# An audio tower on one core: the expert gate's product with its operands exchanged

## The reference

```python
x = hidden_states.reshape(n, d)                  # n = 8000 frames, d = 192, layer-normed
scores = jax.nn.sigmoid(x @ gate_weight.T)       # 8000 x 16
capacity = math.ceil(n / E * TOP_K)              # 1000 frames for each of 16 experts
topk_score, topk_ids = jax.lax.top_k(scores.T, capacity)
xg = x[topk_ids]
gate = jax.nn.silu(jnp.einsum('ecd,efd->ecf', xg, Wg))
up = jnp.einsum('ecd,efd->ecf', xg, Wu)
out = jnp.einsum('ecf,edf->ecd', gate * up, Wd)
out = out * topk_score[..., None]
y = jnp.zeros((n, d), x.dtype).at[topk_ids.reshape(-1)].add(out.reshape(-1, d))
```

## Time and profile before

| | |
|---|---|
| median of 3 runs | 2032.82 us (2029.86 to 2035.56) |
| profiled execution | 2029.4 us, of which 2027.7 us span from the first to the last instruction |
| mean granted TensorE clock | 0.987 |
| the tower in it | to about 1096.5 us |
| a round with all five stages | 31.33 us |

### The profile page before, as it was taken

The page is one execution under the profiler, slowest core; times in us unless marked ns, Lnnn a source line. Parts: engine busy times, 40 slices in busy tenths (PEclk is TensorE's granted clock), DMA queues, the critical chain, the costliest instruction groups (busy, mean ns, idle before and its releaser), DMA issues. The chain is left out here.

```text
span 2027.7 us, 47599 instructions
## 1 busy us (share of the span) xinstructions
PE 1883.7 (93%) x13428; PEld 1605.2 (79%) x13428; DVE 1496.1 (74%) x3956; ACT 1243.6 (61%) x2924; POOL 745.1 (37%) x587
## 2 busy tenths in 40 slices
PE   3899999999999999999985889899999999999997
PEld 2688888888888878888874777688888888888886
DVE  1578788788787887877874777678877778877753
ACT  2687878878878788787862222255555555555553
POOL 0022222122222222222220000357767777776763
PEclk9899999999999999999997999899999999999999
DMA  5556667666666666666664333425544555544452
GB/s 158 151 160 182 179 171 192 167 179 180 171 182 175 173 189 168 178 179 170 188 169 114 108 100 102 115 47 112 97 83 82 96 87 94 109 91 82 84 99 21
DMA packets 318050, 272.97 MB, mean 135 GB/s; under 512 B 80732, under 2 KB 305326, under 8 KB 317998
## 3 DMA queue, kind: packets, MB, share of 16 engines
q1 hardware_dynamic: 238878, 235.53, 43.5%
q0 software_dynamic: 70656, 30.65, 10.3%
q10 hardware_dynamic: 8464, 6.15, 1.0%
HBM read 151.25 MB, written 120.54 MB: 134 GB/s over the span
## 5 line engine op out<-in xcount | busy, mean ns | idle before, releaser
L1217 POOL DMA_INDIRECT ff_xg<-xs_d,ff_idxg x128 | 252.3, 1971 | 244.4 <-issue 232.4
L1230 POOL DMA_INDIRECT out<-ff_y,ff_idxs x128 | 256.8, 2006 | 176.5 <-DVE ff_y L1543 129.1
L524 ACT ACTIVATE sb_prob<-sb_ssb,sb_mx 125x250 f32<-125x250 f32 x512 | 253.1, 498 | 61.7 <-DVE sb_rinv L614 33.7
L1654 PE MATMUL ffp_g<-ff_xsp,ff_wsp 128*128 128x500 f32 x960 | 249.3, 390 | 1.6 <-DVE ff_xsp L1398 1.6
L1654 PE MATMUL ffp_u<-ff_xsp,ff_wsp 128*128 128x500 f32 x960 | 250.5, 391 | 0.0
L1671 PE MATMUL ffp_d<-sh_s_w_room,ff_h_top 128*125 128x384 f32 x768 | 229.6, 362 | 2.7 <-DVE ff_y L1543 2.7
L822 PE MATMUL ps_qps<-sb_hsp,sb_wsp 128*128 128x250 f32 x1280 | 186.6, 293 | 31.8 <-DVE sb_hsp L728 22.9
L1298 ACT ACTIVATE ff_sg<-ffp_g 128x500 f32<-128x500 f32 x192 | 112.7, 587 | 165.9 <-PE ffp_g L1654 163.4
L1654 PEld LDWEIGHTS ffp_u<-ff_xsp,ff_wsp 128*128 128x128 f32 x960 | 180.1, 189 | 40.8 <-DVE sh_s_xraw L1528 4.8
L1654 PEld LDWEIGHTS ffp_g<-ff_xsp,ff_wsp 128*128 128x128 f32 x960 | 180.8, 189 | 37.6 <-issue 1.9
L822 PEld LDWEIGHTS ps_qps<-sb_hsp,sb_wsp 128*128 128x128 f32 x1280 | 161.5, 193 | 57.0 <-ACT sb_rsb L510 28.9
(11 more groups left out here) (203 smaller groups left out, 4047.7 us busy)
## 6 DMA issues: line engine op xcount, KB each, us to landing
bias_d<-sb_rsb SPq DMA_DIRECT2D x256, 219.6 KB
sb_bsk<-bias_d SPq DMA_DIRECT2D x256, 218.8 KB
hx_d<-sb_hx SPq DMA_DIRECT2D x32, 336.0 KB
sb_hxl<-hx_d SPq DMA_DIRECT2D x32, 336.0 KB
ff_wd<-WdT SPq DMA_DIRECT2D x16, 576.0 KB, 5.0
xs_d<-sb_xs SPq DMA_DIRECT2D x32, 238.0 KB
bias_d<-sb_rsb SPq DMA_DIRECT2D x256, 25.5 KB
sb_bsk<-bias_d SPq DMA_DIRECT2D x256, 25.4 KB
```

Of the source, the lines that this page charges most:

```text
L524: a.activation(prob[:, s % 2, t], ssb[:, s % 2, t], ACT.Exp, bias=mx[:, s % 2, t:t + 1], scale=-1.0, accum_out=rs[:, t, s:s + 1]).then_inc ...
L1217: g.indirect_dma_start(xg[:, t], None, xs_d[:, :], bass.IndirectOffsetOnAxis(idxg[:, t:t + 1], 0), bounds_check=last).then_inc(gat[t // HT ...
L1230: g.indirect_dma_start(out_d[:, :], bass.IndirectOffsetOnAxis(idxs[:, t:t + 1], 0), y[:, t], None, bounds_check=last, compute_op=ALU.add). ...
L1654: ins = m_(ps[n % 2][:], wsp[:, i, wk, m * 128:(m + 1) * 128], xsp[:, xp, xk, half * HALF:(half + 1) * HALF], start=k == 0, stop=k == 4)
```

## The change

The gate's product now has the gate's weights as its stationary operand and the frames as the moving one, so that the scores come out expert by expert: 16 partitions of 250 frames in place of 125 partitions of 2 x 16. ACT's exponential, DVE's addition and DVE's reciprocal work on that shape, and the reciprocal writes `scT`. Two products with the identity then bring the scores into the frames' rows, and DVE copies them into `xs`. Before, the reciprocal wrote into `xs`, and two transposes brought the scores into the expert layout. SP's write of the rows now waits for that copy, POOL's write of `scT` for the reciprocal.

```diff
--- before.py
+++ after.py
@@ -189,7 +189,7 @@
         d_y = sb("d_y", [TP, NT])
         xs = sb("xs", [TP, NT, SROW])
         xnT = sb("xnT", [KD, NK, FRAMES])
-        sige = sb("sige", [TP, NT, EXPERTS])
+        sige = sb("sige", [EXPERTS, FRAMES])
         scT = sb("scT", [EXPERTS, FRAMES])
 
         sps = [pb(f"sps{i}", [TP, NT, FRAMES]) for i in range(2)]
@@ -376,7 +376,7 @@
                     if bd is not None and s == 4:
                         sl = bass.ds(bd * FRAMES, FRAMES)
 
-                        apart(sp, READY, (d_ev, D_USES * bd + 2), (c_sg, 2 * bd + 2), (x_dup, bd + 1))
+                        apart(sp, READY, (d_ev, D_USES * bd + 3), (x_dup, bd + 1))
                         sprayed(sp, h1_d[sl, :].rearrange("(t p) n -> p t n", p=TP), h1[:], c_st)
                         sp.dma_start(xnT_d[:, sl].rearrange("(k p) n -> p k n", p=KD), xnT[:]).then_inc(c_st, 16)
                         sprayed(sp, xs_d[sl, :].rearrange("(t p) n -> p t n", p=TP), xs[:], c_st)
@@ -447,7 +447,7 @@
                         pool.wait_ge(d_ch, D_CHAIN * bc + 5)
                         g.tensor_tensor(d_y[:], d_v[:], power[:, 0:NT], ALU.pow).then_inc(d_ch, 1)
                     if bd is not None and s == 4:
-                        pool.wait_ge(d_ev, D_USES * bd + 3)
+                        pool.wait_ge(c_sg, 2 * bd + 2)
                         g.dma_start(scT_d[:, bass.ds(bd * FRAMES, FRAMES)], scT[:]).then_inc(scT_st, 16)
                     if bt is not None and s == 5:
 
@@ -512,7 +512,7 @@
                         a.preload_act_table_set(EXP_SET)
                     if bd is not None and s == 2:
                         act.wait_ge(d_mm, D_USES * bd + 2)
-                        a.activation(sige[:], cps[0:TP, 0:NT * EXPERTS].rearrange("p (t n) -> p t n", t=NT), ACT.Exp, scale=-1.0).then_inc(d_ev, 1)
+                        a.activation(sige[:], cps[0:EXPERTS, 0:FRAMES], ACT.Exp, scale=-1.0).then_inc(d_ev, 1)
                     if bb_ is not None:
                         n = HEADS * bb_ + s
                         for t in range(NT):
@@ -672,14 +672,14 @@
                         dve.wait_ge(d_ev, D_USES * bd + 2)
                         v.tensor_scalar(sige[:], sige[:], 1.0, None, ALU.add).then_inc(c_sg, 1)
                         dve.wait_ge(c_sg, 2 * bd + 1)
-                        v.reciprocal(xs[:, :, 256:SROW], sige[:]).then_inc(c_sg, 1)
+                        wait(dve, scT_st, 16 * bd)
+                        v.reciprocal(scT[:], sige[:]).then_inc(c_sg, 1)
                     if bc is not None and s == 3:
                         dve.wait_ge(c_ch, C_CHAIN * bc + 2)
                         v.tensor_scalar(c_v[:], ss[:], 1.0 / D, EPS, ALU.mult, ALU.add).then_inc(c_ch, 1)
                     if bd is not None and s == 3:
                         dve.wait_ge(d_mm, D_USES * bd + 3)
-                        wait(dve, scT_st, 16 * bd)
-                        v.tensor_copy(scT[:], cps[0:EXPERTS, 0:FRAMES]).then_inc(d_ev, 1)
+                        v.tensor_copy(xs[:, :, 256:SROW], cps[0:TP, 0:NT * EXPERTS].rearrange("p (t n) -> p t n", t=NT)).then_inc(d_ev, 1)
                     if bc is not None and s == 3:
                         dve.wait_ge(c_ch, C_CHAIN * bc + 4)
                         for t in range(NT):
@@ -866,7 +866,9 @@
                         m(tps[0:2 * BINS, 0:FRAMES], dft[:], frames[:], start=True, stop=True).then_inc(t_mm, 1)
                     if bd is not None and s == 1:
                         pe.wait_ge(d_ev, D_USES * bd + 1)
-                        natural(cps[0:TP, 0:NT * EXPERTS].rearrange("p (t n) -> p t n", t=NT), xnT, gate, d_mm)
+                        for k in range(NK):
+                            ins = m(cps[0:EXPERTS, 0:FRAMES], gate[:, k], xnT[:, k], start=k == 0, stop=k == NK - 1)
+                        ins.then_inc(d_mm, 1)
                     if bt is not None and s == 2:
                         pe.wait_ge(t_ev, T_USES * bt + 1)
                         m(tps[0:MELS, 0:FRAMES], mel[:], sq[:], start=True, stop=True).then_inc(t_mm, 1)
@@ -888,7 +890,7 @@
                         if bc is not None:
                             pe.wait_ge(c_ev, C_USES * bc + 1)
                         for t in range(NT):
-                            ins = nc.tensor.transpose(cps[0:EXPERTS, t * TP:(t + 1) * TP], xs[:, t, 256:SROW], ident[0:TP, 0:TP])
+                            ins = m(cps[0:TP, t * EXPERTS:(t + 1) * EXPERTS], scT[:, t * TP:(t + 1) * TP], ident[0:EXPERTS, 0:EXPERTS], start=True, stop=True)
                         ins.then_inc(d_mm, 1)
                     if bt is not None and s == 4:
                         pe.wait_ge(t_ev, T_USES * bt + 2)
```

## The result

| | before | after |
|---|---|---|
| median of 5 runs, us | 2032.82 (2029.51 to 2035.56) | 2049.42 (2044.16 to 2053.72) |
| profiled execution, us | 2029.4 | 2046.4 |
| tower ends at | 1096.51 | 1113.56 |
| a round with all five stages | 31.33 | 31.81 |

A forecast was written before the change was run, and what follows sets the result against it. PE nearly fills a round (30.27 of 31.33 us), but late handovers push it. 15.1 us for 28 full rounds plus 5.6 for the last four, on 2029.4, gave 2050, or 2053 as median; range 2040 to 2067.

The forecast's parts named there:

- The reciprocal: DVE's reciprocal on rows of 250 elements: 1.75 us at 6.4 ns for each further element, +1.40 over before.
- rival of eight cycles an element: DVE's reciprocal takes 2.2 us, the chain is 1.0 later a round, the time 2069; chance 0.07.
- rival of a price by elements in all: DVE's reciprocal stays near 0.35 us, L608's slack takes the rest; with cheaper PE columns 2026; chance 0.05.
- L608's lateness: DVE's L608 starts 1.74 us later, behind the longer exponential, addition and reciprocal.
- slack of L608: Between L608 and ACT's L524 1.01 us are free, and idle time on ACT gives back another 0.19.
- PE is thus 0.16 later at L917, which waits 0.54 for L692 anyway; that wait hides it: PE's own growth costs nothing in a full round; unhidden it would cost 28 x 0.16 = 4.5 us.
- +0.03 and +0.13: PE's growth a round: +0.03 us for the gate's product in slot 1, +0.13 for the second layout in slot 3.
- The 0.54 a round: The chain from L608 through L524 and L692 into PE is 0.54 us late in each of 28 full rounds, 15.1 together.
- The gate's product: PE, slot 1: two products of 250 moving columns hold PE 0.90 us, at most 1.00, against 0.87 before.
- Outside the full rounds: The last four rounds cost 5.6 us together, 4 to 8: 1.57 in the second, 2.4 in the last, 0.8 in each other.
- absorbed: The chain's 0.54 disappears; only PE's 0.16 a round and part of the last rounds stay, 2037; chance 0.10.
- No slack at all: L608's lateness goes on in full, 1.74 x 28 + 5.6 = 54 us, 2087; chance 0.04.

The follow-up runs named there:

- e2: The kernel before plus one reciprocal of 16 x 250 ones behind L675, into a tile nobody reads; ratio 1.0043, a round of 31.46 us.
- e11: The kernel before plus one reciprocal of 16 x 110 ones behind L675, into a tile nobody reads; 2032.02 us in one run, a round of 31.32.
- e8: The kernel before plus one reciprocal of 16 x 375 ones behind L675, into a tile nobody reads; 2062.33 us in one run, a round of 32.26.
- e1: The changed kernel with the sigmoid made by tanh and one DVE operation, without addition and reciprocal; ratio 1.006, a round of 31.82 us.
- e9: e7 with the reciprocal moved on DVE in slot 3 behind L608, ahead of L618; ratio 1.005, a round of 31.53 us.
- e10: The kernel before with mel filters widened to 128 columns and the DCT's stationary tile to 128 rows; ratio 0.9948, a round of 31.01 us.
- e7: The changed kernel with the gate's weights widened by zeros to 128 columns and the score tile to 128 rows; ratio 1.007, a round of 31.67 us.

## Why the prediction was right, and where it wasn't

The direction and the size came out: 2049 for 2053, and 31.81 us a round for 31.87. By its steps:

- **The reciprocal** took 1703 ns for the 1.75 us predicted. From 32 to 250 elements that is 6.2 ns each, the slope of the first lengths. Those had 125 partitions and this has 16, so having fewer partitions saves nothing. The rival of eight cycles an element, 2.2 us, is refuted, and with it the figure worked out from the repeat count on the page of the Trainium skill (VectorE: DVE Perf Modes, First, the fixed hardware budget). The rival of a price by elements in all is refuted too: e2 and e11 have it at 1645 and 770 ns.
- **Exponential and addition:** 353 and 279 ns for 0.37 and 0.35. The addition was over-estimated by 0.07.
- **L608's lateness:** 1.83 for 1.74, of which 0.17 is PE's delay in slot 1, which I had not sent down this way. DVE and ACT's own part is 1.66.
- **The slack of L608:** 1.40 for 1.20. Its first part is 1.04, not 1.01, since L524 starts 0.38 behind L608 here. ACT gives back 0.20 at L532, near the 0.19 that I took, and 0.16 more between L532 and L542, where I had not looked (in e8 the one is 1.09 late, the other 0.93).
- **The failed step is "PE is thus 0.16 later at L917, which waits 0.54 for L692 anyway; that wait hides it".** The two terms, +0.03 and +0.13, measured 0.17 and 0.31, and they are not hidden. L692 is itself behind PE: L844 of slot 3 releases L510, and from there the same chain leads to L917. The predicted idle time of PE ahead of L917 does not appear either; L919 starts 0.44 behind L784 (0.46 before). e1 shows PE's growth alone giving the full 0.49. The 0.54 a round that I put down to the reciprocal is 0.43 by the rule, and it lies under PE's 0.49; without PE's 0.17 in it, it would be 1.66 - 1.40 = 0.26. My sum was right to 0.06 by luck: it counted one way into the round and put the other at nothing, and the larger of the two, which alone counts, happens to be nearly what I gave the first.
- **The gate's product** held PE 0.95 where my estimate from the rule for isolated products, with two records a product, made 0.43 us (the Trainium skill, TensorE: Matmul & The Clock Gate, Back-to-back issue gap); the row of L866 was the better guide, but I took 0.90 and not its 1.00, and left out that the product would also start 0.09 later.
- **Outside the full rounds** the profile has 17.05 - 28 x 0.48 = 3.6 us for the 5.6 predicted. The last four stretches, counted as under e9, take 30.28, 26.60, 21.79 and 24.65 us: +0.88, +1.15, +0.36 and +0.39, together 2.8, where I had 0.8, 1.57, 0.8 and 2.4. The other 0.8 lie ahead of the first product with `w1`, before the changed stage has run at all; that product stands anywhere from 116.4 to 121.9 in the profiles. The last round is the term that was badly sized. In it, POOL's write of `scT` (before, and now):

```profile
1090.46 0.55 POOL L451 DMA_DIRECT2D scT_d<-sb_scT  x1 [5.54 <-DVE sb_scT L682]
```

```profile
1107.65 0.55 POOL L451 DMA_DIRECT2D scT_d<-sb_scT  x1 [6.07 <-DVE sb_scT L676]
```

The tower ends 6.05 behind this write before and 5.91 now (5.86 in e1, 5.95 in e9). The write no longer waits for the second layout and its copy, which gives back most of the reciprocal's 1.35. The write of `xs` that I charged with 0.65 starts 6.07 ahead of the tower's end before and 3.61 now, so it does not set it. Over the four stretches the profiles of kernels with a long reciprocal of 250 elements have 2.8 to 6.3 us more than before, those with the hyperbolic tangent between 1.5 less and 1.5 more. So the reciprocal costs at the ends, where little covers it; how much of the larger sums is the lower clock isn't separated.
- **The other rivals:** "absorbed" supposed that PE's growth stays and is small; it stays and is three times as large. "No slack at all" fails by e11.

What stays open: why a load with few rows or columns does not start early. The runs show it for 16 and 40 columns and for 16 and 41 rows; L891 of the old kernel, with 16 columns, did start 0.07 ahead, and no run looked for the boundary. The tile ahead matters as well. Before, the load of 125 x 128 behind the DCT's 41 x 125 starts together with its own product (522.11); in e10, where the DCT's has 128 rows, the same load starts 0.16 ahead (515.45 and 515.61).

## What to carry to other kernels

When two chains meet in one ring, undo each cause alone before putting the loss down to either: PE's growth alone costs 0.49 a round (e1), the longer DVE and ACT operations alone would cost 0.26 by the rule (0.13 was measured in e2, where L608 is 0.12 less late), and both together cost 0.48. "That wait hides it" holds only if the awaited work doesn't itself start from the engine that became late, so follow the releaser's own chain back to its start. And before exchanging a product's operands, look at what the new stationary tile measures: a small one gives fewer elements to load and still costs PE time, while padding it lengthened no round in the runs here.

## What the hardware showed unexpectedly

- A product whose stationary tile has 16 or 40 columns, or 16 or 41 rows, starts 0.09 to 0.10 us later behind its predecessor than the same one padded to 128 (L870 0.59 and 0.50, L872 0.53 and 0.43), and behind three of the four the next product also starts sooner once it is padded (0.55 and 0.32 us behind the mel filters, 0.53 and 0.46 behind the second layout).
- A load of 96 x 16 takes 97 ns a record and one of 96 x 128 195, yet e7, with the longer loads, has a shorter round than the changed kernel (31.67 and 31.81).
- The reciprocal's price from 2 to 375 elements a partition (166, 248, 353, 770, 1645, 2430 ns) rises by 5.3 to 6.6 ns an element. The first three lengths have 125 partitions and the others 16; the same 250 elements took 1703 ns as L676.
- A releaser in the trace can be a coincidence. Before, the load for L822 in slot 2 is marked with a wait of 0.39 us for ACT's L510; in e10 L510 stands where it stood (7.57 us from the round's start, 7.56 before), and L822 starts 0.32 sooner.
